# First ids by a DMA on ACT's queue, layer 1's dense parts moved, and a PSUM bank per tile, in a DLRM tower on one core

## The reference

```
e = stack([tbl_f[ids[:, f]] for f in 26])             # 512 x 26 x 128
c = concat([e, r_dense_x[:, None, :]], axis=1)        # 512 x 27 x 128
z = einsum('bfd,bgd->bfg', c, c)[:, upper triangle]   # 512 x 351 pairs
h = concat([z, r_dense_x], axis=1)                    # 512 x 479
h = maximum(h @ W_top1 + b_top1, 0)                   # 512 x 512
h = maximum(h @ W_top2 + b_top2, 0)                   # 512 x 256
y = h @ W_top3                                        # 512 x 1
```

## Time and profile before

| | |
|---|---|
| time, median of 3 runs | 104.04 us (104.0, 104.04, 105.1) |
| the profiled execution's own time | 103.44 us |
| its span, first to last instruction | 101.6 us |
| granted TensorE clock | 1.00 of full speed |
| PE busy | 92.5 us (91%) |
| POOL / DVE / ACT busy | 61.6 / 61.0 / 59.7 us |
| DMA | 13.37 MB, mean 132 GB/s |

### The profile page before, as it was taken

The page is one execution under the profiler, slowest core; times in us unless marked ns, Lnnn a source line. Parts: engine busy times, 40 slices in busy tenths (PEclk is TensorE's granted clock), DMA queues, the critical chain, the costliest instruction groups (busy, mean ns, idle before and its releaser), DMA issues.

```text
span 101.6 us, 3386 instructions
## 1 busy us (share of the span) xinstructions
PE 92.5 (91%) x1452; PEld 75.7 (74%) x1452; DVE 61.0 (60%) x97; ACT 59.7 (59%) x113; POOL 61.6 (61%) x69
## 2 busy tenths in 40 slices
PE   3979798999999999999999889998899989999990
PEld 3948474868877676868887889788787869968870
DVE  2499799999999999999694320046200470036201
ACT  5099999999999999999942014005440045403040
POOL 3777777777777777787777777777777730000000
DMA  1669999997889758899922221221122210000000
GB/s 48 210 230 242 230 233 224 224 240 223 176 245 254 246 158 209 195 236 351 346 65 58 52 58 52 58 58 52 52 58 58 52 52 6 0 6 6 0 0 1
DMA packets 6716, 13.37 MB, mean 132 GB/s; under 512 B 2031, under 2 KB 3311, under 8 KB 6702
## 3 DMA queue, kind: packets, MB, share of 16 engines
q1 hardware_dynamic: 4718, 9.10, 33.2%
q0 software_dynamic: 1984, 4.07, 15.6%
HBM read 13.16 MB, written 0.00 MB: 129 GB/s over the span
## 4 chain that ended last, share of the span: by engine, by line
PE 48%; DVE 27%; issue 11%; ACT 7%; DMA 3%; SPq 1%; DVEq 0%; ACTq 0%
DVE onehot L568 16%; PE ps_gram L321 13%; PE ps_h L357 11%; DVE table_lo L557 8%; PE ps_h L298 6%; PE ps_h L379 6%; DMA table_raw<-in_tbl 3%; PE ps_h L352 3%; ACT away L463 3%; PE ps_tp L308 3%; PE ps_gram L298 3%; PE ps_tp L379 2%; ACT table_hi L454 2%; DVE zT L601 1%; DVE gramT L585 1%
## 5 line engine op out<-in xcount | busy, mean ns | idle before, releaser
L263 POOL DMA_INDIRECT rows<-in_tbl,ids_sb x62 | 60.8, 981 | 20.0 <-issue 18.6
L568 DVE TENSOR_TENSOR onehot<-ids_bc,ps_h 125x1536 fp32r<-125x1536 int16 (+2 forms) x20 | 32.2, 1610 | 0.0
L298 PE MATMUL ps_gram<-onehot,table_hi 125*128 125x512 f32 x72 | 28.9, 414 | 2.0 <-DVE onehot L568 1.6
L298 PE MATMUL ps_gram<-onehot,table_lo 125*128 125x512 f32 x72 | 27.4, 397 | 0.2 <-DVE table_lo L557 0.2
L490 ACT COPY featT<-ps_tp 128x512 f32<-128x512 f32 (+3 forms) x18 | 10.2, 588 | 15.7 <-PE ps_tp L308 15.6
L298 PEld LDWEIGHTS ps_gram<-onehot,table_hi 125*128 125x128 f32 x72 | 13.4, 188 | 8.0 <-DVE onehot L568 4.6
L298 PEld LDWEIGHTS ps_gram<-onehot,table_lo 125*128 125x128 f32 x72 | 13.5, 188 | 3.6 <-DVE table_lo L557 0.8
L557 DVE TENSOR_TENSOR table_lo<-table_raw,table_hi 125x512 fp32r<-125x512 f32 x22 | 15.0, 687 | 1.5 <-ACT table_hi L454 1.5
L463 ACT ACTIVATE away<-ids_bc,vnr 125x512 f32<-125x512 int16 (+1 forms) x22 | 14.3, 718 | 0.0
L321 PE MATMUL ps_gram<-featT 128*26 128x26 f32 x1024 | 13.2, 193 | 0.9 <-issue 0.3
L321 PEld LDWEIGHTS ps_gram<-featT 128*26 128x26 f32 x1024 | 11.0, 107 | 4.0 <-issue 3.3
(11 more groups left out here) (50 smaller groups left out, 65.9 us busy)
## 6 DMA issues: line engine op xcount, KB each, us to landing
table_raw<-in_tbl SPq DMA_DIRECT2D x11, 448.0 KB
w<-in_W SPq DMA_DIRECT2D x6, 256.0 KB
ids_bc<-in_ids_lookup SPq DMA_DIRECT2D x10, 128.0 KB, 5.7
rows<-in_tbl,ids_sb POOLq DMA_INDIRECT x62, 4.0
table_raw<-in_tbl SPq DMA_DIRECT2D x11, 52.0 KB
denseT<-in_denseT SPq DMA_DIRECT2D x1, 256.0 KB, 4.2
b2w<-in_b2w SPq DMA_DIRECT2D x1, 256.0 KB
ids_sb<-in_ids SPq DMA_DIRECT2D x1, 52.0 KB, 1.8
```

The costliest lines, as they stand in the source:

```text
L263: nc.gpsimd.indirect_dma_start(out=rows[:, t % ROWB, n, :], out_offset=None, in_=tables[f], in_offset=bass.IndirectOffsetOnAxis(ap=ids_sb[ ...
L298: last = nc.tensor.matmul(table_bank[k][:, at:B], (table_hi, table_lo)[part][:, k % 2, c, :], onehot[:, k % 2, c, at:B], start=n == 0, sto ...
L568: nc.vector.tensor_tensor(onehot[:, k % 2, c:end, at:B], ids_of(k, 0).rearrange("k (o b) -> k o b", o=1).broadcast_to(part), row.rearrange ...
```

## The change

It does five things. (1) Table 0's ids come spread out by a DMA like those of the other tables, issued as ACT's first instruction; DVE's cast, PE's eight broadcast matmuls and their two semaphores go, PE's warm-up is 12 matmuls in one piece, and ACT writes its one-hot chunks of table 0 before it splits the table, not after. (2) Layer 1 of a tile has a PSUM bank of its own (`h1_of`), alternating by tile, except the last tile, which still has its halves in the two banks; `relu1` of tiles 0 to 2 is one piece. (3) The dense parts of layer 1 stand one place earlier: tile 0's after lookup 6, tile 1's in tile 0's place, tile 2's in tile 1's, half of tile 3's in tile 2's, the other half at the end. For this `denseT` is loaded after table 4 instead of after table 7, the dense part of W1 after table 5 instead of at the end, and ACT's copy of the dense features is split in two. (4) Both late lookups (k = 9 and 10) write the bank `ps_h2`, so lookup 10 waits for the copy of lookup 9. (5) Two of tile 2's transposed groups stand before `gram(1, 0)`, the rest of tile 2's and tile 3's are spread otherwise.

```diff
-WARM = 8
+WARM = 12
+DENSE_AFTER = 6
-        table_bank = [ps_gram[:, k % 2, :] for k in range(FULL)] + later_bank
+        table_bank = [ps_gram[:, k % 2, :] for k in range(FULL)] + [ps_h2_bank] * (NL - FULL)
+        def h1_of(t, n):
+            if t < TILES - 1:
+                return ps_h1[t % 2][:, n, :]
+            return ps_h1[1 - n // (C1 // 2)][:, n % (C1 // 2), :]
@@ sync
-                if k == FULL - 2:
+                if k == RAW + 1:
                     sp.dma_start(denseT[:, :, :], denseT_in.rearrange("d (t p) -> d t p", p=P)).then_inc(dense_in, 16)
+                if k == RAW + 2:
+                    sp.dma_start(w1[:, ZC, :], W1[:, ZC, :]).then_inc(w1_dense_in, 16)
@@ tensor
-            keep_busy(WARM // 2)
-            broadcast_first_ids()
-            keep_busy(WARM // 2)
+            keep_busy(WARM)
             for k in range(FULL):
                 lookup(k)
                 for n in GROUPS_AFTER.get(k, []):
                     transpose_group(n)
+                if k == DENSE_AFTER:
+                    layer1_dense(0)
             lookup(FULL + 1)
+            transpose_group(FIRST[2])
             transpose_z(0)
-            dense(0)
+            layer1_dense(1)
+            transpose_group(FIRST[2] + 1)
             pairs(0)
             gram(1, 0)
             layer2(0)
             gram(1, 1)
-            dense(1)
-            for n in range(FIRST[2], FIRST[3] - 1):
-                transpose_group(n)
+            layer1_dense(2)
+            transpose_group(FIRST[2] + 2)
             transpose_z(1)
-            transpose_group(FIRST[3] - 1)
+            transpose_group(FIRST[2] + 3)
             pairs(1)
             ...
-            dense(2)
+            layer1_dense(TILES - 1, range(C1 // 2))
             transpose_group(FIRST[3])
             transpose_group(FIRST[3] + 1)
             transpose_z(2)
-            transpose_group(FIRST[3] + 2)
             pe.wait_ge(zT_done, TILES - 1)
             for c in range(ZC):
-                layer1_pairs(2, 0, c)
-            transpose_group(FIRST[3] + 3)
-            for c in range(ZC - 1):
-                layer1_pairs(2, 1, c)
-            transpose_group(FIRST[3] + 4)
-            layer1_pairs(2, 1, ZC - 1)
+                layer1_pairs(2, c)
+                transpose_group(FIRST[3] + 2 + c)
             t = TILES - 1
             gram(t, 0)
@@ scalar
+            act.dma_start(ids_bc[:, 0, :], spread(0)).then_inc(bc_in[0], 16)
-            split_hi(0)
             write_away(0)
             write_onehot(0)
+            split_hi(0)
             write_away(1)
             split_hi(1)
```

More of the change, by code:

```diff
@@ L211, in spread_ids @@
             def spread_ids(k):
[L212 removed]
+                sp.dma_start(ids_bc[:, k, :], spread(k)).then_inc(bc_in[k], 16)
             def load_w1(c):
@@ L272, in keep_busy @@
                 for _ in range(count):
-                    nc.tensor.matmul(ps_z[:, 0:ZC, :], ident_r[:, :],
+                    nc.tensor.matmul(ps_h1[0][:, 0:ZC, :], ident_r[:, :],
                                      ident_r[:, :].rearrange("k (o p) -> k o p", o=1).broadcast_to([P, ZC, P]),
                                      start=True, stop=True)
[L277 to L283, removed]
             def lookup(k):
@@ L354, in layer1_pairs @@
-            def layer1_pairs(t, half, c):
-                for n in range(C1 // 2):
-                    m = slice((half * C1 // 2 + n) * P, (half * C1 // 2 + n + 1) * P)
-                    last = nc.tensor.matmul(ps_h1[half][:, n, :], w1[0:ZK, c, m], zT[0:ZK, c, t % 2, :],
-                                            start=False, stop=n == C1 // 2 - 1 and c == ZC - 1)
+                    pe.wait_ge(dense_in, 16)
+                    pe.wait_ge(w1_dense_in, 16)
+                elif 2 <= t < TILES - 1 or columns[-1] < C1 // 2:
+                    pe.wait_ge(h1_relu, C1 * (t - 1))
+                elif t == TILES - 1:
+                    pe.wait_ge(h1_relu, C1 * t)
@@ new lines, in layer1_dense, with layer1_pairs @@
+                for n in columns:
+                    nc.tensor.matmul(h1_of(t, n), w1[:, ZC, n * P:(n + 1) * P], denseT[:, t, :],
+                                     start=n == 0 or t == TILES - 1 and n == C1 // 2, stop=False)
+            def layer1_pairs(t, c, columns=range(C1)):
+                for n in columns:
+                    last = nc.tensor.matmul(h1_of(t, n), w1[0:ZK, c, n * P:(n + 1) * P], zT[0:ZK, c, t % 2, :],
+                                            start=False, stop=c == ZC - 1 and n == columns[-1])
@@ L433, in _ @@
             gram(t, 1)
-            dense(t)
+            layer1_dense(t, range(C1 // 2, C1))
             bias_last()
@@ L444, in _ @@
                 for half in range(2):
-                    layer1_pairs(t, half, c)
+                    layer1_pairs(t, c, range(half * C1 // 2, (half + 1) * C1 // 2))
             layer2(t)
```

108 lines of the change are left out of this document (46 added, 62 removed).

## The result

The changed kernel took 105.75 us (median of 20 runs, 104.58 to 108.19), the kernel before 104.2 us (20 runs, 103.09 to 105.38): a ratio of 1.0163, with a 95% interval from 1.0132 to 1.0195. So the change costs 1.7 us. Part of that is at the start, where the first ids came later (5.1 us after issue) than in every other trace of this start (4.2 to 4.5 us).

The account below looks back on a forecast made before the run. One-hots and splits on DVE and ACT bound the first stage, to about 44 us, PE the second. Terms -0.5 + 0.15 + 0.4 - 0.25 + 0.9 = +0.7 on the median 104.04 gave 104.8 us, range 103.3 to 105.9.

Parts of the forecast that it names:

- three signs of being wrong: Table 1's low half before 10.3, ACT's casts of tables 5 or 6 waiting for DMAs, tile 2's part not 0.75 us longer.
- those that were to show it: Trace signs expected, among them ACT's first Abs on the ids at about 3.4 and table 1's low half at about 10.7.
- The start: Table 0's ids by DMA, landing at 3.4, let ACT and DVE begin sooner: 0.5 us won, between 0 and 0.88.
- fourth rival: At the start, ids land after 5.1 us, so DVE and ACT start later than before: about 105.5 us, chance 0.05.
- Tile 3's rows come in time, for POOL is well ahead: In tile 2's place, POOL's gathers of tile 3's rows were claimed to hold nothing up; no cost was given.
- Tile 0's dense part after lookup 6: Its 8 instructions ahead of lookup 7, mostly hidden in PE's waits for one-hots: 0.15 us lost, between 0 and 0.4.
- The early loads: denseT and W1 loaded ahead of tables 5 and 6: costed at nothing; as a rival 106.0 us, chance 0.13.
- Tile 0's place: Before tile 0's pairs, two groups of transposes come in and a wait for a copy goes: 0.4 us lost.
- Tile 1's place: Between gram and tile 1's pairs two groups of transposes leave, but most becomes a wait for DVE: 0.25 us won.
- Tile 2's place: A group of four among tile 2's pairs and a last group copied before tile 3's gram: 0.9 us lost.
- The end: After tile 3's gram half a dense part less, but PE's wait for ACT grows by as much: nothing.
- The tile terms: The four terms for tile 0's dense part and the places of tiles 0, 1 and 2: together 1.2 us lost.

Follow-up runs that it names:

- b1_start: Kernel before with only the new start (table 0's ids by ACT's DMA, chunks before cast, 12 warm-up matmuls in one piece): 105.18 us, ratio 1.0163.
- b2_tail: Changed kernel with the old start (ids by PE's broadcast, cast first), all else as changed: 106.38 us, ratio 1.0203 to the kernel before.
- b3_warm: Changed kernel with 22 warm-up matmuls instead of 12, to keep PE busy until lookup 0: 106.57 us, ratio 1.0289 to the kernel before.
- b4_best: Changed kernel with the old start and each group of transposes put where PE waits for DVE: 103.46 us, ratio 1.0021 to the kernel before.

## Why the prediction held, and which of its steps didn't

The time lies in the range (103.3 to 105.9), 0.95 us above the forecast, and slower by over 1%, to which I gave 0.37. It got there with one term of the wrong sign and one that was missing. None of its three signs of being wrong came, but two of those that were to show it failed: ACT's first Abs on the ids stood at 5.90, not 3.4, and the low half of table 1 at 12.12, not 10.7.

- **The start, "0.5 us won"**: 1.7 us lost when made alone (b1_start). The step that failed is the landing of the new DMA, "the low end is the other early DMA, 1.8 us". That row held only because it was alone on its way; with a second queue both took 3.8 to 5.1 us, in every trace that has it. Why two loads side by side take so long is open. My fourth rival, ids after 5.1 us, is what the traces show in part: at 5.02 in b1_start, at 5.91 in the profile after. Its chance of 0.05 was too small, and it had the price of DVE's delay alone.
- **"Tile 3's rows come in time, for POOL is well ahead"**: true for the changed kernel, where the group at 90.16 doesn't wait, but with the old order it was ahead by less than it lost. Before, the gather issued at 80.02 had landed after 2.5 us, and its group was transposed at 85.66, so it was 3.2 us ahead. In b1_start the same gather was issued at 83.06, 3.0 us later, and took 4.2 to land, hence the 1.28 us of waiting at 87.34. I had priced `ids_sb` only as DVE's input. POOL starts on the same load and has no pause in 62 gathers to catch up in.
- **Tile 0's dense part after lookup 6, 0.15 us**: on its spot it costs nothing (PE has no wait ahead of lookups 7 and 8 any more). But its eight matmuls move the end of a block of code, and the wait in lookup 10 grew from 0.29 to 1.36 us. This is the missing term, about 1.1 us, of which 0.9 is left by the end of lookup 10 (12.11 against 11.23 us from the end of lookup 8); no row showed it, and the 0.29 us of before was in the chain under "issue", which I had passed over.
- **The early loads, nothing**: right; no cast waited for a DMA.
- **Tile 0's place, 0.4 us**: 2.10 us in place of 1.79, so 0.3.
- **Tile 1's place, 0.25 us won**: 0.54 won (71.17 to 74.56 is 3.39 us, where 3.93 stood). I had taken tile 2's DVE chain for tile 1's; there DVE began 0.42 us after PE went on (83.02 to 83.44 in the chain), here 0.12 (71.17 to 71.29).
- **Tile 2's place, 0.9 us**: 0.88 (86.72 to 90.80 is 4.08 us, where 84.06 to 87.26 is 3.20), with the wait for the copy of one row as told. **The end, nothing**: 7.58 us from the last gram to DVE's last step (95.54 to 103.12) for 7.60 (92.20 to 99.80).

The tile terms together are 0.6 us, a half of the 1.2 forecast, and the wait for code brings them to 1.7 to 2.0, against 2.1 measured by b2_tail. The two halves of the change cost 1.7 and 2.1 us alone and 1.7 together. That the time fell into the range is luck in part: the start went 2.2 us the wrong way and the wait for code was unforeseen, and most of this was hidden where the two losses overlap.

How they overlap is seen in how late each profiled execution is against the profile before, in us (b2_tail's holds the half clock in lookup 10):

| kernel | end of lookup 8 | end of lookup 9 | end of lookup 10 | tile 3's first gram | end |
|---|---|---|---|---|---|
| changed | 1.83 | 1.88 | 2.72 | 3.54 | 3.32 |
| b1_start | 0.41 | 1.52 | 0.83 | 1.91 | 1.53 |
| b2_tail | 0.20 | 0.26 | 3.04 | 3.65 | 3.53 |
| b3_warm | 0.20 | 1.95 | 1.90 | 3.07 | 3.00 |
| b4_best | 0.00 | 0.03 | 0.91 | -0.13 | 0.06 |

In b1_start and b3_warm PE comes to tile 1's rows with little loss and waits there for POOL; in the changed kernel it comes to them at 48.66, after the gather that b1_start had to wait for until 48.52, and has no such wait. To tile 3's group of two it comes at 89.21, and that group's last gather, issued at 83.90, had landed after 3.8 us. What PE loses in the lookups and the tiles is the cover under which POOL's delay disappears. That is read from the rows and not tested by a run of its own.

## What to carry to other kernels

A load that is ready early because it is alone does not stay early when a second queue starts beside it: price a new DMA at the start by the loads that it delays, and follow each of those to all its readers, the gathering engine too. An engine whose list has no pauses carries a late start to its end, so look how far ahead of its reader each landing is, not at its busy share. And where a short wait without a releaser stands in PE's chain behind a run of very short matmuls, note its distance in instructions: code put in ahead of it moves it, and a saving of a microsecond can go there.

## What the runs showed of the hardware

- A 52 KB load and a 128 KB load issued at the same time on two queues landed after 3.8 and 4.2 us (b1_start) and 4.7 and 5.1 us (the profile after, by its first reader and its landing), the 52 KB one after 1.8 us when the second queue was silent.
- After 2.6 to 3.4 us of idle time PE's lookup matmuls followed each other at 0.43 us (3.60 to 3.75 us for the first eight), and at 0.23 without the idle time (2.08 for the eight). In b1_start the granted clock was 0.50 there, the lower of the two levels, after 2.91 us without a matmul, and 1.00 after it. The profile after shows 1.00 from 9.30 to 12.80, with the same spacing, so there the spacing is the better witness. Windows of b1_start:

```profile
8.30:11.70 3.40, 3.29 (x8) 2.64 (x9) 3.40 (x5) 3.40 (x7) 2.49 (x4) 0.50 1.06 254
11.70:15.00 3.30, 3.30 (x16) 2.73 (x15) 2.98 (x4) 3.26 (x6) 2.69 (x3) 1.00 1.01 239
```

- 62 indirect gathers of 128 rows run on POOL back to back, mostly at 1.25 us each (0.94 and 0.30 to the next); 8 to 11 of them take 1.1 to 1.5 us in place of 0.94, most of these while the tables are loaded. The start of the first to that of the last is 78.5 us before and 79.7 in b1_start.
- PE waits 0.17 to 1.68 us at a place that is a number of instructions and not an operation, and goes on 1.4 to 1.6 us after a 16 KB packet on the instruction queue has ended.
